# First layer of a two-layer graph network: one of three bf16 weight products moves from VectorE to GpSimd

## The reference

```python
h = relu(layernorm(x))
h = proj(expmap0(h))
for W, b in ((W0, b0), (W1, b1)):
    h = hyp_linear(h, W, b)                        # 64x64 product, row-wise scaling
    xt = logmap0(h)
    agg = segment_sum(xt[src] * w[:, None], dst)   # the sum over edges
    h = hyp_act(proj(expmap0(agg)))
x = x + h
h = relu(layernorm(x))
# edge network: relu([h[src], h[dst]] @ W1 + b1) @ W2 + b2, mean over dst; added to x
```

## Time and profile before

| what | value |
|---|---|
| median of 3 runs | 1554.04 us |
| the profiled execution: its own time | 1557.46 us |
| its span, first to last instruction | 1555.7 us |
| mean granted TensorE clock, share of full | 0.846 |
| PE busy | 1169.3 us (75%) |
| DVE busy | 952.4 us (61%) |
| POOL busy | 484.4 us (31%) |
| ACT busy | 355.9 us (23%) |

### The profile page before, as it was taken

The page is one execution under the profiler, slowest core; times in us unless marked ns, Lnnn a source line. Parts: engine busy times, 40 slices in busy tenths (PEclk is TensorE's granted clock), DMA queues, the critical chain, the costliest instruction groups (busy, mean ns, idle before and its releaser), DMA issues.

```text
span 1555.7 us, 43807 instructions
## 1 busy us (share of the span) xinstructions
PE 1169.3 (75%) x17976; PEld 1109.1 (71%) x17976; DVE 952.4 (61%) x1294; ACT 355.9 (23%) x657; POOL 484.4 (31%) x424
## 2 busy tenths in 40 slices
PE   0427887787787887389986328888898998898885
PEld 0327777777777775389985128888888897898885
DVE  6689999999999991645542315544345344353421
ACT  0122332323223331200012502222122222121220
POOL 1000000000000000100000633777787777787760
PEclk9868999999999997599965559899799979799975
DMA  2002222222222224099900254554454544545420
GB/s 78 0 1 98 96 96 96 96 105 111 96 96 96 96 96 192 1 329 365 374 2 24 95 135 128 143 140 129 126 132 127 140 113 132 148 112 132 110 60 21
DMA packets 59111, 181.58 MB, mean 117 GB/s; under 512 B 29696, under 2 KB 29897, under 8 KB 58767
## 3 DMA queue, kind: packets, MB, share of 16 engines
q1 hardware_dynamic: 46076, 154.35, 28.4%
q0 software_dynamic: 12992, 26.63, 7.7%
HBM read 128.17 MB, written 52.76 MB: 116 GB/s over the span
## 4 chain that ended last, share of the span: by engine, by line
DVE 24%; POOL 24%; PE 24%; issue 17%; DMA 5%; DVEq 2%; ACT 2%; SPq 0%; POOLq 0%; ACTq 0%
POOL arena L537 24%; PE PS L1317 8%; DVE arena L982 8%; DVE arena L960 3%; PE PS L1302 3%; DVE arena L967 2%; PE PS L1341 2%; DMA arena<-q_table 2%; PE PS L1283 2%; PE PS L1388 2%; DMA q_table<-arena 1%; PE PS L1259 1%; PE PS L1438 1%; DVEq L349 1%; DVE arena L949 1%
## 5 line engine op out<-in xcount | busy, mean ns | idle before, releaser
L537 POOL DMA_INDIRECT arena<-p_table,idx x406 | 474.0, 1167 | 409.0 <-DMA idx<-in_src 278.5
L1317 PE MATMUL PS<-arena,A 125*64 125x72 f32 x5100 | 210.3, 243 | 120.2 <-DVE aggTw L992 94.5
L1317 PEld LDWEIGHTS PS<-arena,A 125*64 125x64 f32 x5100 | 194.6, 150 | 130.9 <-issue 60.1
L1462 PE MATMUL PS<-arena 128*128 128x72 f32 x1250 | 188.2, 301 | 74.7 <-ACT arena L694 74.7
L1450 PE MATMUL PS<-arena 125*128 125x128 bf16 x1875 | 204.4, 231 | 51.1 <-DVE arena L1192 51.1
L1462 PEld LDWEIGHTS PS<-arena 128*128 128x128 f32 x1250 | 173.3, 215 | 77.9 <-ACT arena L694 68.3
L547 POOL MEMSET RT<- 1x3197 f32 x1 | 2.8, 2754 | 609.7 <-PE PS L1388 609.7
L1450 PEld LDWEIGHTS PS<-arena 125*128 125x128 bf16 x1875 | 151.0, 107 | 52.1 <-issue 50.4
L694 ACT ACTIVATE arena<-PS 128x512 f32<-128x512 f32 (+1 forms) x175 | 94.1, 549 | 402.6 <-PE PS L1452 401.9
L982 DVE TENSOR_TENSOR arena<-arena,slots 128x1800 bf16<-128x1800 bf16 x153 | 159.2, 1110 | 0.0
L1302 PE MATMUL PS<-arena 128*128 128x72 bf16 x3825 | 142.6, 203 | 4.0 <-DVE arena L982 4.0
(11 more groups left out here) (193 smaller groups left out, 1682.3 us busy)
## 6 DMA issues: line engine op xcount, KB each, us to landing
adjacency<-arena SPq DMA_DIRECT2D x51, 900.0 KB, 3.6
arena<-adjacency SPq DMA_DIRECT2D x51, 900.0 KB, 5.9
Bw<-slot_rows SPq DMA_DIRECT2D x25, 781.2 KB
Cw<-slot_rows SPq DMA_DIRECT2D x25, 675.0 KB
arena<-offset_rows SPq DMA_DIRECT2D x26, 432.0 KB
arena<-p_table,idx POOLq DMA_INDIRECT x406
arena<-q_table SPq DMA_DIRECT2D x153, 18.0 KB
q_table<-arena SPq DMA_DIRECT2D x1, 2343.8 KB
```

Source lines behind the costliest of these rows:

```text
L537: pool.indirect_dma_start(GP[k][:, t, :], None, p_d[:, :], bass.IndirectOffsetOnAxis(ap=idx[k][:, t:t + 1], axis=0))\
L1317: last = mm(sums[half, :], A[:, b, :], adjacency[0:PN, b, :], start=(b < 2), stop=(b >= NB - 2))
L1462: last = mm(rs_ps, Hs[:, b, :], Os[k][:, b, :], start=(b == 0), stop=(b == NB - 1))
```

## The change

GpSimd gets a loop over the groups in the first layer. For each group it waits for the fields (`slots_set`), for the one-hot `OD` (`dst1_set`) and for the matmuls that read the same `WD` buffer two groups ago, and then multiplies `OD` with the third weight part into `WD[k][:, 2]`. VectorE's loop does only parts 0 and 1. A new semaphore, `third_set`, is waited for in three places: by VectorE before it overwrites `OD` for the next group, by ScalarE before it overwrites `slots[k]` two groups later, and by TensorE before `blocks`.

```diff
+            def third_weights(g, k, n):
+                pool.wait_ge(slots_set, nth(g))
+                pool.wait_ge(dst1_set, nth(g))
+                pool.wait_ge(blocks_done[-1], nth(g - 2))
+                nc.gpsimd.tensor_tensor(
+                    WD[k][:, 2].rearrange("p b (w d) -> p b w d", d=2), OD.rearrange("p b (w d) -> p b w d", d=2),
+                    slots[k][:, 4, 0:NB, :].unsqueeze(2).broadcast_to([128, NB, HW, 2]), ALU.mult)\
+                    .then_inc(third_set, 1)
+
+            fast = in_order(pool, 0)
+            with pool.If(fast == 1):
+                groups(pool, third_weights)
             fast = in_order(pool, 1)
...
             def take_slots(g, k):
                 sc.wait_ge(slots_done, nth(g))
                 sc.wait_ge(onehots_set, nth(g - 2))
+                sc.wait_ge(third_set, nth(g - 2))
...
             def slot_destinations(g, k):
 
                 ve.wait_ge(slots_set, nth(g))
+                ve.wait_ge(third_set, nth(g - 1))
...
             def slot_weights(g, k):
 
                 ve.wait_ge(dst1_set, nth(g))
-                for c in range(3):
+                for c in range(2):
...
             def blocks(g, k):
 
                 pe.wait_ge(onehots_set, nth(g))
+                pe.wait_ge(third_set, nth(g))
```

More of the change, by code:

```diff
@@ L257, in gnn_kernel @@
                                 "slots_done", "slots_set"))
-        dst1_set, onehots_set = counts("dst1_set"), counts("onehots_set")
+        dst1_set, onehots_set, third_set = counts("dst1_set"), counts("onehots_set"), counts("third_set")
         blocks_done, blocks_set = (counts(n, len(CHUNKS)) for n in ("blocks_done", "blocks_set"))
```

## The result

The changed kernel takes 1638.42 us (median of 4 runs, 1636.04 to 1640.87); before it was 1554.06 us on the same chip (4 runs, 1551.33 to 1563.87). The ratio is 1.0543, 95% interval 1.0491 to 1.0595: 84 us slower. The forecast was 1696 us and +142, range 1595 to 1775. The direction and the mechanism were right and the time lies inside the range, but the loss is 58 us smaller than forecast.

A forecast was written before the change was run, and what follows sets the result against it. VectorE was taken to bound the first layer at 9.46 us a group; losing 1.00 us but being held by GpSimd's 4.1 us product gave +158 or +125 us, middle +142, so 1696 us, range 1595 to 1775.

The forecast's parts named there:

- The bound: First layer: VectorE, busy for all 474.8 us, sets the period of 9.46 us a group; TensorE has 20% of slack.
- The removal: First layer: one of three VectorE weight products of 1.00 us leaves each of 51 groups, -51 us.
- The waits cost nothing: The waits for `third_set` in the first layer cost 0 so long as GpSimd's product stays under 6 us.
- T: Moment in each first-layer group when `dst1_set` comes, at the end of VectorE's L967; the prediction counts the later waits from it.
- The exclusion in both directions: First layer: a VectorE step reading two SBUF tensors and GpSimd's product block each other, whichever starts first; forecast case, chance 0.72.
- the gather: Sign from the edge network: a GpSimd gather took 3.31 us beside a two-input VectorE product, 0.94 with no VectorE work beside it.
- D: Duration of GpSimd's product of 128 x 1800 bf16 per group: 4.1 us taken, bounds 1.6 to 5.2, forecast case from 2.65.
- the select: One-input GpSimd instruction, 293 ns for 128 columns; gave 1.41 ns a column, plus 0.83 for a second stream, 2.24.
- A: GpSimd gets in behind L974 and holds the first L982 for all of D: period 12.56 us, +158 us.
- B: GpSimd comes in behind the last L982, runs 0.64 us beside L992 and L949, then holds L930: period 11.92, +125 us.
- the rival of a slow TensorE: First layer: TensorE, idle over 4 us a group, drops to 1.2 GHz and binds: period 15.4, 1857 us; chance 0.07 with D above 5.2.
- TensorE's share: Sign: TensorE's busy share of the first layer falls from 80% to near 62%, its clock below 0.92.

## Why the prediction was right, and where not

- **The bound.** VectorE's 9.46 us period as the bound of the stage: right. Taking 1.00 us off it without more gives 8.46 us and -54 us in the total.
- **The removal, 51 x 1.00 us:** right, by that same run.
- **The waits cost nothing:** right, by that run too. One figure in it was off: with a period of 8.46 us VectorE asks for `third_set` at T + 7.5, not T + 8.4, which changes nothing.
- **The exclusion in both directions:** right, and shown: L996 or L943 are stretched by what GpSimd works, a clear that reads nothing holds nobody, a copy that reads one tile holds for its 1.5 us, and steps with an input in PSUM run on. The forecast had one direction only from the gather.
- **D, the mis-sized term.** The prediction took 4.1 us from 2.24 ns a column. It is 3.20 us alone, and the hold is 3.0 us, inside its bounds of 2.65 and 5.2. From 5 buckets (0.79 us) to 25 (3.20) it grows by 2.41 us in 1440 columns: 1.67 ns a column and 0.19 us fixed. The select's 293 ns for 128 columns was too short an instruction to take a rate from: a copy of 1800 columns reads one input too, and holds for 1.5 us, 0.83 ns a column, which is the clear's rate, not the select's 1.41. With 0.83 for each of two streams it would have been 0.11 + 1800 x 1.66 ns = 3.1 us. The error of 1.1 us x 51 = 56 us is nearly the whole distance between +142 and +84. So the term that was mis-sized is the rate taken from the select.
- **Orders A and B.** Both were named, and the middle was taken, with no reason for an even split; that they alternate, so that the middle is right, was luck. With 3.0 us, A gives 8.46 + 3.00 = 11.46, as seen. B gives 8.46 + 2.37 for L943 = 10.83, as seen. In seven groups, the shown one among them, L962 starts late (0.40 us behind L1006 in place of 0.14): it waits for `prefix` on TensorE, which ran near its lower clock level behind 5.69 us of idle time (the 50 passes took 3.38 us). This costs nothing: L943 is then shorter by as much (2.11 us of hold and 0.26 of lateness), since the product ends when it ends. So the rival of a slow TensorE shows in single steps, but is worth 0 in the period.
- **TensorE's share** fell to 71% of the stage, not 62%. With before's 378 us it would be 68% in 558 us, as the stage grew less than forecast; the rest is its busy time of 399 us at 0.85 of the clock.
- The Trainium skill's rule (SBUF — State Buffer, section Who interferes with whom) was borne out in both directions. Its narrower note (Advanced Engine Details and Errata, section Mode Summary), by which only two-port modes would block, was not: by it the time would have been 1503 us. The Trainium skill's rate for GpSimd (GPSIMD Engine Reference, section Elementwise — side-by-side cycle accounting; 3.95 us by the estimate) was nearer than the prediction's own, and still too long by 0.75 us.

## What to carry to other kernels

Before moving an elementwise step from a full VectorE to an idle GpSimd, compare GpSimd's duration, not its idleness, with what VectorE saves: where VectorE's neighbours read two SBUF tensors, each microsecond in which GpSimd reads is taken off VectorE, here 1.67 ns a column given for 0.52 saved. No VectorE step was stretched beside ScalarE in these runs, and it was the better place, although it needs one instruction per bucket. A duration on GpSimd holds its waiting as well: read its length from where the VectorE step ahead ends, or from a run in which nothing stands in its way.

## What was not expected of the hardware

The two orders alternate from group to group without exception (51 of 51 in the changed kernel), also with the buffers exchanged, with half of the columns, and with a copy. In one order GpSimd gets in between two VectorE steps that follow each other without a gap, in the other it stands behind three in a row. And TensorE's granted clock in the stage went with the length of its waits for `add_sums` more than with its busy share: 0.85 with the product on GpSimd (waits up to 5.7 us, 71% busy), 0.92 before (2.56 us in the earlier trace rows, 80%), 0.99 in the version with the whole third part off VectorE (up to 1.1 us, 82%).
